# A two-layer gated block: rows that carry x through the first experts, and the dispatch matrices of the second on VectorE

## What is computed

```python
x = x + tanh(g_xattn[0]) * attention0(layernorm(x), ctx, mask)   # 16 heads of 8
x = x + tanh(g_ffn[0])   * experts0(layernorm(x))
x = x + tanh(g_xattn[1]) * attention1(layernorm(x), ctx)
x = x + tanh(g_ffn[1])   * experts1(layernorm(x))

def experts0(x):                       # 8 experts, hidden 512, the best one for each token
    top1 = argmax(x @ Wg.T)
    return gelu(x @ W1[top1] + b1[top1]) @ W2[top1] + b2[top1]

def experts1(x):                       # 16 experts, hidden 64, the two best for each token
    p = softmax(x @ w_router)          # 8 places for each expert in each sequence
    # the first 8 tokens that chose expert e are its rows, the others are dropped
    # out = sum over both choices of p * (silu(r @ gate[e]) * (r @ fc[e])) @ proj[e]
```

## Time and profile before

| | |
|---|---|
| runs | 547.47, 554.09, 555.18 us (median 554.09) |
| profiled execution | 551.82 us |
| its span, first to last instruction | 549.9 us |
| mean granted TensorE clock | 0.932 |
| DMA | 30.40 MB |

### The profile page before, as it was taken

How to read it: one execution, slowest core, us unless ns; L and a number is a source line. 1 busy time by engine, 2 the same in 40 slices (tenths; PEclk the granted TensorE clock), 3 DMA queues, 4 the chain that set the end, 5 groups by cost and what they waited for, 6 DMA issues and landing times.

```text
span 549.9 us, 17402 instructions
## 1 busy us (share of the span) xinstructions
PE 480.2 (87%) x6027; PEld 363.6 (66%) x6027; DVE 390.2 (71%) x1185; ACT 318.5 (58%) x761; POOL 272.0 (49%) x325
## 2 busy tenths in 40 slices
PE   2789999999989886999965879999898988998997
PEld 1456777777766785999953556767676756754554
DVE  5678878988777766455525778889998668566555
ACT  2445564665764674677735546656766365556553
POOL 2532534536463258888884426343534143544455
PEclk9999999999998898999995899999999789579999
DMA  6115334322110144555335032010000000000112
GB/s 194 48 52 151 87 89 117 86 76 74 40 51 16 37 128 77 83 90 72 36 35 173 2 77 68 15 32 21 3 12 2 2 2 2 1 1 2 39 50 69
DMA packets 50469, 30.40 MB, mean 55 GB/s; under 512 B 12240, under 2 KB 46800, under 8 KB 50384
## 3 DMA queue, kind: packets, MB, share of 16 engines
q1 hardware_dynamic: 31760, 16.97, 11.1%
q0 software_dynamic: 6640, 4.67, 6.5%
q10 hardware_dynamic: 11984, 7.64, 5.1%
HBM read 19.41 MB, written 9.85 MB: 53 GB/s over the span
## 4 chain that ended last, share of the span: by engine, by line
PE 57%; issue 13%; DVE 11%; POOL 9%; ACT 5%; DMA 2%; ACTq 2%; DVEq 1%; SPq 0%; POOLq 0%
PE T_ps L847 9%; PE A_ps L860 9%; PE S_ps L836 6%; POOL x_mid L1123 6%; DVE maxes L583 4%; PE Q_ps L817 3%; PE S_ps L830 3%; PE Q_ps L753 3%; PE X_ps L876 3%; PE f_H_ps L1175 2%; PE Q_ps L742 2%; PE m_T_ps L1460 2%; PE m_X_ps L1447 2%; PE f_Y_ps L1189 2%; DVE prob L591 2%
## 5 line engine op out<-in xcount | busy, mean ns | idle before, releaser
L583 DVE TENSOR_REDUCE maxes<-S_ps 128x8 f32<-128x512 f32 x128 | 87.6, 684 | 44.2 <-PE S_ps L836 44.0
L410 POOL TENSOR_TENSOR k_blk<-kT,col_a 128x512 f32<-128x512 f32 x64 | 67.6, 1067 | 90.8 <-ACT kT L471 63.3
L513 ACT ACTIVATE probT<-T_ps 128x512 f32<-128x512 f32 x128 | 76.0, 594 | 53.1 <-PE T_ps L847 49.4
L847 PE MATMUL T_ps<-col_a,prob 128*128 128x128 f32 x512 | 86.0, 293 | 9.8 <-DVE prob L591 5.9
L591 DVE TENSOR_TENSOR prob<-S_ps,maxes 128x512 f32<-128x512 f32 x128 | 88.5, 692 | 4.4
L847 PEld LDWEIGHTS T_ps<-col_a,prob 128*128 128x128 f32 x512 | 59.1, 147 | 48.4 <-issue 36.3
L860 PEld LDWEIGHTS A_ps<-v_blk,probT 128*64 128x64 f32 x2048 | 66.5, 141 | 10.9 <-issue 10.8
L860 PE MATMUL A_ps<-v_blk,probT 128*64 128x18 f32 x2048 | 72.9, 215 | 0.0
L1123 POOL DMA_INDIRECT x_mid<-f_out,f_rows x39 | 60.9, 1562 | 12.1 <-issue 10.7
L836 PE MATMUL S_ps<-k_blk,qT 32*64 32x256 f32 x1024 | 47.1, 426 | 4.1 <-DVE prob L591 3.5
L988 DVE TENSOR_TENSOR f_hid<-f_H_ps,f_b 128x512 f32<-128x512 f32 x39 | 27.0, 692 | 33.3 <-PE f_Y_ps L1189 28.7
(11 more groups left out here) (199 smaller groups left out, 924.6 us busy)
## 6 DMA issues: line engine op xcount, KB each, us to landing
f_w<-in_W ACTq DMA_DIRECT2D x16, 256.0 KB, 2.8
ctxT<-in_ctxT SPq DMA_DIRECT2D x12, 256.0 KB, 2.8
f_rows<-sorted_rows SPq DMA_DIRECT2D x39, 64.5 KB, 1.9
out<-m_final SPq DMA_DIRECT2D x32, 64.0 KB, 1.6
x_all<-in_x SPq DMA_DIRECT2D x6, 256.0 KB, 5.0
x_mid<-x_all SPq DMA_DIRECT2D x6, 256.0 KB, 2.7
x_all<-x_mid SPq DMA_DIRECT2D x6, 256.0 KB, 3.5
ctxT<-in_ctxT SPq DMA_DIRECT2D x8, 128.0 KB, 2.3
```

Source lines behind the costliest of these rows:

```text
L410: nc.gpsimd.tensor_tensor(k_blk[:, t % 2, :, :, :], kT[:, g.at(R), t - g.first, :].rearrange("p (b k) -> p b k", b=2).unsqueeze(2).to_broa ...
L513: nc.scalar.activation(probT[:, t % 2, 4 * h:4 * h + 4, :], T_ps[:, :, :], ACT.Exp, scale=SCALE).then_inc(probT_ready, 1)
L583: nc.vector.tensor_reduce(maxes[:, t % 2, h, :, :], half_of(h), X, ALU.max).then_inc(max_ready, 1)
L847: last = nc.tensor.transpose(T_ps[:, j, :], pair, ident[:, :])
```

## The change

A row that is scattered now carries x and its normalized row side by side, in one tensor `token_rows` of 257 floats a row (x 128, normalized 128, index 1). `x_all` and `r_xn` are views of it. So the rows that come back for a tile hold x too: VectorE adds b2 to it (`residual`, two steps behind the load), finish adds the product's result to that, and the send is a plain indirect write of finished rows. `keep` and its waits go. Finish needs no expert's number any more, residual loads it. SyncE writes six of the eight ends' pads, ScalarE two, one number later than before. The pads are cleared by 15 memsets on GpSimd at numbers 4 to 18, numbered at 20 and written out at 22. In the second layer `low`, the exponentials by tile and the split in 24 and 8 tiles go: `lower` (VectorE, 128x512) at number 71, one exponential of all gaps and one of all logits (ScalarE) at 72, `add_up` (VectorE, 128x512) at 73. `one` is made by VectorE just ahead of `dispatch`, with two buffers, and waits for its own result in between; GpSimd has no step there.

```diff
-RW = D + 1
+RW = 2 * D + 1
...
-            def keep(g):
-                sp.wait_ge(y_added, g.i + 1)
-                sp.dma_start(r["x_mid"][dram_rows(g), :].rearrange("(u p) d -> p u d", p=P), x_group(g)).then_inc(kept[g.own >= FULL_GROUPS], 16)
...
                 pool.indirect_dma_start(r["sorted"], bass.IndirectOffsetOnAxis(ap=row[:, t:t + 1], axis=0),
-                                        r_xn[:, t, :], None).then_inc(scattered[t >= FULL_FROM][t % 4], 16)
+                                        token_rows[:, t, :], None).then_inc(scattered[t >= FULL_FROM][t % 4], 16)
...
-                nc.gpsimd.tensor_scalar(low[:, at], r["top"][:, at, 0], -1.0, None, ALU.mult).then_inc(gap_ready, 1)
...
-            def raise_(g):
-                act.wait_ge(gap_ready, 2 * (g.own + 1))
-                nc.scalar.activation(r["gap"][:, g.local:g.local + g.n], r["gap"][:, g.local:g.local + g.n], ACT.Exp).then_inc(raised_done, 1)
-                for t in range(g.local, g.local + g.n):
-                    if t > 1:
-                        act.wait_ge(raised_done, t + g.own)
-                    nc.scalar.activation(raised[:, t % 2, :], r["logits"][:, t, :], ACT.Exp, bias=low[:, t:t + 1],
-                                         accum_out=r["total"][:, t:t + 1]).then_inc(raised_done, 1)
+            def raise_all(_):
+                act.wait_ge(gap_ready, NG)
+                act.wait_ge(lowered, 1)
+                nc.scalar.activation(r["gap"][:, :], r["gap"][:, :], ACT.Exp).then_inc(raised_done, 1)
+                nc.scalar.activation(r["logits"][:, :, :], r["logits"][:, :, :], ACT.Exp).then_inc(raised_done, 1)
...
+            def lower(_):
+                dve.wait_ge(top_ready, NT)
+                nc.vector.tensor_tensor(r["logits"][:, :, :], r["logits"][:, :, :], r["top"][:, :, 0:1].to_broadcast([P, NT, E1]),
+                                        ALU.subtract).then_inc(lowered, 1)
+            def add_up(_):
+                dve.wait_ge(raised_done, 2)
+                nc.vector.tensor_reduce(r["total"][:, :], r["logits"][:, :, :], X, ALU.add).then_inc(summed, 1)
...
-        def finish(t):
+        def residual(t):
+            need_table(dve, t)
             e = dve.value_load(entry(1, t), min_val=0, max_val=E0 - 1)
...
             if t >= DEEP:
                 dve.wait_ge(sent[t % DEEP], 16 * (t // DEEP))
-            vec.tensor_tensor(out[:, t % DEEP, :], Y_ps[t % 2][:, 0:D],
-                              b2[:, bass.ds(e, 1), :].rearrange("p a c -> p (a c)"), ALU.add).then_inc(y_out, 1)
-        return [(bias, 1), (finish, 3)]
+            dve.wait_ge(rows_in[t % RINGS], 16 * (t // RINGS + 1))
+            vec.tensor_tensor(out[:, t % DEEP, :], rows[:, t % RINGS, 0:D],
+                              b2[:, bass.ds(e, 1), :].rearrange("p a c -> p (a c)"), ALU.add).then_inc(x_biased, 1)
+        def finish(t):
+            dve.wait_ge(y_ready, t + 1)
+            dve.wait_ge(x_biased, t + 1)
+            vec.tensor_tensor(out[:, t % DEEP, :], Y_ps[t % 2][:, 0:D], out[:, t % DEEP, :], ALU.add).then_inc(y_out, 1)
+        return [(bias, 1), (finish, 3), (residual, 2)]
...
-        return [(load(sp), range(FULL_TILES), lambda t: FULL_AT + 2.5), (pad_ends(sp, range(0, E0, 2)), once, lambda _: REST_AT)]
+        return [(load(sp), range(FULL_TILES), lambda t: FULL_AT + 2.5), (pad_ends(sp, range(6)), once, lambda _: REST_AT)]
...
-                                    out[:, t % DEEP, :], None, compute_op=ALU.add).then_inc(sent[t % DEEP], 16)
+                                    out[:, t % DEEP, :], None).then_inc(sent[t % DEEP], 16)
...
-        return [(warm, once, lambda _: NT - 0.5)] + placed(sooner, 0.1) + [(pad_ends(eng, range(1, E0, 2)), once, lambda _: REST_AT)] + placed(later)
+        return [(warm, once, lambda _: NT - 0.5)] + placed(sooner, 0.1) + [(pad_ends(eng, range(6, E0)), once, lambda _: REST_AT + 1)] + placed(later)
...
         def move(t):
+            known(dve, t)
+            vec.tensor_scalar(one[:, t % 2, :], iota, sent[:, 0, t:t + 1], None, ALU.is_equal).then_inc(one_ready, 1)
+            wait(dve, moved, t - RING + 1)
             dve.wait_ge(one_ready, t + 1)
-            wait(dve, moved, t - RING + 1)
...
+        def clear(n):
+            nc.gpsimd.memset(r0["pads"][:, n, :], 0.0).then_inc(r0["pads_cleared"], 1)
```

123 lines of the change are left out of this document (48 added, 75 removed).

## The result

The changed kernel takes 551.65 us (median of 20 runs, 548.96 to 565.94), the kernel before 547.44 (20 runs, 543.74 to 556.79). The ratio is 1.0099, 95% interval 1.0074 to 1.0124: 1% slower, where I had forecast some 1.5% faster. The ratio takes fast runs alone, those within 1.5% of the fastest of their kernel, and so isn't the quotient of the two medians (1.0077). The profiled execution took 552.37 us with a span of 550.5. The first profile of before (551.82) was of an execution above the middle: 15 of the 20 runs of before lie under 551.

A forecast was written before the change was run, and what follows sets the result against it. TensorE, busy 480.2 of 549.9 us, was taken as the bound, where it stands or its clock is low. 551.82 + 0 - 0.7 (drain) - 2.4 (second experts) - 3.0 (clock) = 545.7, said as 546; 8-in-10 range 536 to 558.

The forecast's parts named there:

- Steady first experts, term 0: First experts: VectorE's queue turns over in 1.80 us, below TensorE's 1.90, if it runs ahead; 0, bounds 0 and +12.
- (c): Rival: VectorE's queue becomes the bound of the first experts, 0.47 us for each of 26 tiles, 558 us; chance 0.11.
- (d): Rival: residual meets the send on a shared port in the first experts, +10 us, 556; chance 0.05.
- Send, kept writes, end of the experts, term 0: First experts and their end: send about 1.0 us and hidden, x's kept writes not waited for; 0, end bounds 0 and -1.2.
- Drain, term -0.7: Drain of the first attention: up(8) starts near 214, tile 13's rows land near 227.4; -0.7 us, bounds -2.7 and +1.5.
- up(12) later than 229: Drain of the first attention: named sign of a wrong forecast; up(12) was expected near 227.
- The memset, term 0: VectorE's memset goes, no wait of TensorE for it seen; GpSimd's 15 small ones lie in half idle steps; 0.
- m_one, term -1.5 at 421 and -0.7 at 464: Second experts: m_one on VectorE takes 0.28 without hand-over; bounds -0.8 and -1.99 at 421, 0 and -1.9 at 464.
- VectorE's added load, term +1.0: Second experts: 32 x 0.28 = 9.0 us more work on VectorE costs +1.0, bounds 0 and +9.0.
- Gate exponentials, -1.2 at 462: Second layer: they leave the path to m_slotsT, -1.2, at most -1.42; five other groups -0.5, bounds 0 and -6.
- The clock, term -3.0: Second experts, 424 to 434: with the stop cut to some 0.4 the clock stays up; -3.0 us, bounds 0 and -3.3.
- Rival (b): VectorE's added load eats the gain in the second experts, +4 and the clock falls as before, 549 to 557; chance 0.22.

The follow-up runs named there:

- e1: Only the first experts' part of the change, second layer's routing and dispatch as before, against the kernel before: 548.69 us, ratio 1.005.
- f4: Kernel before with VectorE making both halves of all 32 dispatch matrices, nothing else, once more: 545.51 against 547.30 us, ratio 0.9948.
- g4: The kernel before, unedited, run against itself: ratio 0.9997.
- e4: The kernel before, unedited, run once more for a second profile: 548.0 us in its profile.
- e7: Kernel before with only the first experts' part, ScalarE's two pads at number 39, on a slower chip: ratio 1.0126.
- e8: Kernel before with its pads (129 wide) cleared by 15 memsets on GpSimd in place of one on VectorE: ratio 1.0016.
- g1: Kernel before with one exponential for all gates, nothing else, once more: ratio 1.0055.
- g3: Kernel before with only the first experts' part, ScalarE's two pads at number 39, once more: 547.32 against 546.17 us, ratio 1.0047.
- e6: Kernel before with one exponential for all gates, nothing else: ratio 1.0021.
- e2: Only the second layer's part of the change, first experts as before, against the kernel before: 550.60 against 547.98 us, ratio 1.0051.
- e3: Changed kernel with ScalarE's two pads back at number 39, against the kernel before: 550.25 us, ratio 1.0059.
- f3: Kernel before with one exponential, lower half a number later, VectorE's pairs for the first eight matrices only: 547.84 us, ratio 0.9997.
- f1: The changed kernel once more, no further edit, against the kernel before: 549.75 us, ratio 1.0063.
- f2: Changed kernel with ScalarE's two pads at number 39, once more, against the kernel before: 550.12 us, ratio 1.0035.
- g2: Kernel before with the whole of the second layer's part of the change, once more: 547.78 us, ratio 1.0033.
- e5: Kernel before with VectorE making both halves of the dispatch matrices, nothing else, on a slower chip: ratio 0.9961.

## Why the prediction was wrong, point by point

**Steady first experts, term 0: right.** Period 1.90. The queue does run ahead: finish starts 0.61 behind the start of bias and residual's load is hidden behind them. Rivals (c) and (d) fall: VectorE's idle time before bias is 0.66, residual takes 0.29. It was 0.77 before: the 0.29 more cost it 0.11.

**Send, kept writes, end of the experts, term 0: right in sum.** The send measured 0.96 (1.0 said). The xn of the second layer came 0.8 later, not 2.85: some 2 us of the drain's loss were taken back there, where five other profiles with the new rows show 0.2 to 0.9 (the last send starts at 285.88, 1.08 later than before, yet statistics at 290.33, having waited 5.16 us for x in place of 7.70):

```profile
285.88 0.95 POOL L1106 DMA_INDIRECT x_mid<-f_out,f_rows  x1 [0.30 <-issue]
...
290.33 0.49 DVE L595 BATCH_NORM_STATS2 stats<-token_rows 128x6 f32<-128x128 f32 x2 [5.16 <-DMA token_rows<-x_mid]
```

**Drain, term -0.7: this step failed.** The sign that I had named for it, up(12) later than 229, came: 229.20. SyncE's six pads went as I had said (the last issued at 221.15 and done at 221.5, for 221.3), but the landing took 4.93 us where I had at most 4.2, and the load 2.87 with its number where I had 2.5: its rows are there at 228.99 in place of 227.4. Two things I had not asked. What do the two tiles wait for past which I moved ScalarE's pads? The gelu of tile 8 waits for a bias that stands behind VectorE's table steps, so these pads are issued at 220.10 and 221.19, beside SyncE's last ones. And what becomes of TensorE, which starts up(8) 4 us sooner and has nothing to do at the end? It stops for 2.66 us with a low clock behind, 1.6 us for which the sum had no term. The step "ScalarE writes its pads only after turn_out of tiles 8 and 9" was taken as pure gain, and costs. Measured: +2.85 in the first profile; by the means of two profiles against three +3.0 from the counts to the steady part, outside the bounds of -2.7 and +1.5. With the pads early the whole of it is gone from the traces; by run times they are worth 0 to 2 us.

**The memset, term 0: right in sum by luck.** Two effects that I had at nothing nearly cancel, -1.03 behind it at 53.7 and +0.70 at 100: see below.

**m_one, term -1.5 at 421 and -0.7 at 464: mis-sized.** -0.7 at 423.89 and nothing at 464. The wait went, but I let m_dispatch miss its k_blk: it didn't, and took 1.03.

**VectorE's added load, term +1.0, bounds 0 and 9: mis-sized.** Subtracted product by product (changed kernel against e1, which lacks it) 3.3 us: 0.94, 0.50, 1.33 and 0.54 at four waits for m_dispatch, of which 0.4 comes back at 482, where e1 has a wait of its own. The sum of 32 x 0.28 doesn't count as such: a pair takes 0.66 where the group's places are the last thing known. Of the 1.33, f4 has 1.05 without the lower at 128x512, so lower's own part (term +0.5) is 0.3.

**Gate exponentials, -1.2 at 462: right (-1.1).** The five other groups' -0.5 don't show: the difference to before stays at 4.24 from 341 to 420.

**The clock, term -3.0: failed as a step.** I can set the profiles side by side from the first T_ps behind the first dispatch matrix to the first move, the same products in each:

```
                                   stop   clock: 10 us, next 10, rest   us in all
before, g4                         1.99   0.50  0.84  0.98              33.7, 33.8
before (e4)                        2.00   0.66  0.83  1.00              32.9
e1, e7, e8, g1, g3            1.95-1.99   0.50-0.51  0.83-0.84  0.98-1.00   33.6 to 33.7
e6                                 1.95   0.83  0.69  0.86              33.7
changed, e2, e3, f3           1.32-1.33   0.50-0.51  0.84  0.97-0.99    33.7 to 33.8
changed again (f1), f2        1.32-1.33   1.00  0.70  0.85              34.1, 34.2
g2                                 1.32   0.89  0.50  0.77              38.0
both halves on VectorE, f4, e5 1.38,1.36  1.00  0.83  1.00              31.1, 31.1
```

The half of the step that says "with a shorter stop the clock stays up" holds in five of these nine profiles with the short stop, and in one of the nine with the long one (e6). The half that says "then 3 us are won" holds in two, f4 and e5, both of the kernel with the pairs alone, by 2.6; in f1 and f2 the low stretch comes 10 us later and nothing is won, in g2 (a run 5 us above the middle of its kernel), with 0.50 in its second 10 us, the same work takes 4.3 more. And the base was off: I took the 551.82 of one execution, whose second experts ran at 0.51, as the kernel's time, where another of the same kernel shows 0.69 and 548.0.

What keeps f4's clock up where f1's falls? The traces show one difference ahead of the fall, a second stop 7 to 8 us behind the first T_ps. The changed kernel (f1), then the pairs alone (f4):

```profile
425.88 0.69 DVE L1276 TENSOR_SCALAR m_one<-row_constants,r_sent 128x128 f32<-128x128 f32 x1
...
426.60 1.09 DVE L1279 SCALAR_TENSOR_TENSOR m_dispatch<-row_constants,r_sent,m_one 128x128 f32<-128x128 f32 x1
...
431.80 0.63 PE L761 MATMUL X_ps<-col_a,token_rows 128*128 128x128 f32 x4 [1.93 <-DVE token_rows L588]
```

```profile
422.41 0.27 DVE L1293 TENSOR_SCALAR m_one<-row_constants,r_sent 128x128 f32<-128x128 f32 x1
...
422.71 0.86 DVE L1296 SCALAR_TENSOR_TENSOR m_dispatch<-row_constants,r_sent,m_one 128x128 f32<-128x128 f32 x1
...
427.68 0.63 PE L784 MATMUL X_ps<-col_a,r_xn 128*128 128x128 f32 x4 [1.27 <-DVE x_all L610]
```

In f1 the next matrix's m_one and m_dispatch are both drawn out beside GpSimd's work; in f4 GpSimd still has the small `low` there, its larger operation starts 0.3 us later, and m_one is through before it. VectorE is 0.65 earlier, and TensorE stops for 1.27 (1.26 in e5) in place of 1.93 (1.93 in f2, 1.97 in g2). Then the clock is at 0.50 for some 3 us in f4 and e5, for some 10 in f1 and f2, for some 20 in g2. It would also be a reason why the two halves of the second layer's part don't add up: taking `low` away makes the pairs dearer. No run changes this stop alone, so that it decides on the clock is not shown. Rival (b), VectorE's load eats the gain (549 to 557), is what happened in the second layer, with the drain's loss on top.

## What to carry to other kernels

When a step is moved behind others on an engine, look at what those others wait for, not only at how long they take, and at what the engine that is let go sooner will find at the end: the two pads moved past a gelu that waited 4.2 us, and TensorE's stop moved with them to a place with a low clock behind it. Where a result's last consumer needs it at once, count start to start of the whole pair on the engine that takes it over, 0.66 us here, and not its share of busy time. Before a gain is worked out of a low clock in one profile, see whether a second execution of the same kernel has it, and whether it doesn't just come later: here they were worth 4 us from one execution to the next, and two executions with the clock up behind the stop had it low 10 us on. One profile of each kernel isn't enough to call a stretch of low clock the change's.
